# First attention of a hybrid kernel: VectorE takes additions and maxes in another place, and two products of the shared expert move into the last pair

## The reference

```
x = x + attn_a(layernorm(x))          # q, k, v, softmax(q k^T / sqrt(128)) v, w_o
logits = layernorm(x) @ router_w      # 4096 tokens, 8 experts
idx1, idx2 = first and second argmax of softmax(logits)
pos1 = cumsum(mask1) - mask1          # place of a token in its expert, in token order
pos2 = cumsum(mask2) - mask2 + sum(mask1)
expert_in = dispatch @ x              # at most 1280 tokens for an expert
y = combine @ (silu(expert_in @ w1 + b1) @ w2 + b2)
shared = silu(x @ sw1 + sb1) @ sw2 + sb2
x = x + y + 0.1 * shared
```

## Time and profile before

| | |
|---|---|
| median of 3 runs | 773.42 us |
| these runs | 767.63, 775.83, 773.42 us |
| the profiled execution | 770.89 us, span 769.1 us |
| mean granted clock of PE | 0.977 |
| PE busy | 704.7 us, 92% of the span |
| DVE busy | 523.9 us, 68% |
| ACT busy | 449.7 us, 58% |
| POOL busy | 440.9 us, 57% |

### The profile page before, as it was taken

The page is one execution under the profiler, slowest core; times in us unless marked ns, Lnnn a source line. Parts: engine busy times, 40 slices in busy tenths (PEclk is TensorE's granted clock), DMA queues, the critical chain, the costliest instruction groups (busy, mean ns, idle before and its releaser), DMA issues.

```text
span 769.1 us, 18168 instructions
## 1 busy us (share of the span) xinstructions
PE 704.7 (92%) x6152; PEld 641.6 (83%) x6152; DVE 523.9 (68%) x1665; ACT 449.7 (58%) x1144; POOL 440.9 (57%) x564
## 2 busy tenths in 40 slices
PE   6888789799999997889999998999999899999996
PEld 5777689799999996667777776777779899999996
DVE  5877765366556565768888988877676556655536
ACT  2565454344444443677878878787755444456545
POOL 6367777166666651344545767777777265666640
PEclk9999869999999998899999999999999999999999
DMA  7997111455556334333533434333201346555328
GB/s 245 309 323 183 46 48 55 58 113 108 108 99 133 78 104 118 104 99 109 142 101 91 126 119 147 100 95 111 62 30 53 53 84 131 109 97 112 90 68 287
DMA packets 167715, 89.35 MB, mean 116 GB/s; under 512 B 120576, under 2 KB 151890, under 8 KB 167528
## 3 DMA queue, kind: packets, MB, share of 16 engines
q1 hardware_dynamic: 155704, 69.89, 36.6%
q0 software_dynamic: 9216, 17.34, 6.6%
q10 hardware_dynamic: 2704, 0.98, 0.6%
HBM read 49.63 MB, written 39.67 MB: 116 GB/s over the span
## 4 chain that ended last, share of the span: by engine, by line
PE 57%; DVE 5%; POOL 5%; DMA 5%; SPq 4%; issue 4%; ACT 3%; ACTq 0%; DVEq 0%; POOLq 0%
PE bank L940 22%; PE bank L919 19%; PE bank L1021 4%; DMA qc<-qk_rows 3%; SPq L439 3%; POOL x_slots L611 3%; PE bank L980 2%; PE bank L998 2%; PE bank L1002 2%; POOL pt L695 2%; DVE negp L1951 1%; PE bank L976 1%; PE bank L981 1%; ACT pt L1389 1%; PE bank L1040 1%
## 5 line engine op out<-in xcount | busy, mean ns | idle before, releaser
L1291 ACT ACTIVATE hT<-bank,bias_T 128x256 f32<-128x256 f32 x448 | 175.7, 476 | 186.4 <-PE bank L919 186.3
L626 POOL DMA_INDIRECT y_rows<-yo,row_cur x160 | 158.5, 990 | 127.9 <-DVE yo L1845 103.2
L1951 DVE TENSOR_REDUCE negp<-bank 128x2 f32<-128x512 f32 (+1 forms) x192 | 129.6, 685 | 44.3 <-PE bank L981 27.1
L940 PE MATMUL bank<-w_s,hT 128*128 128x128 f32 x1280 | 155.9, 275 | 0.0
L611 POOL DMA_INDIRECT x_slots<-xr,slot_u x128 | 129.9, 1015 | 38.7 <-issue 35.5
L940 PEld LDWEIGHTS bank<-w_s,hT 128*128 128x128 f32 x1280 | 150.0, 192 | 0.0
L919 PE MATMUL bank<-xT_hl,w_hl 128*128 128x256 f32 x960 | 135.4, 291 | 9.1 <-DVE xT_hl L1719 9.1
L695 POOL TENSOR_SCALAR_AFFINE_SELECT pt<-pt 128x512 f32<-128x512 f32 x128 | 86.0, 680 | 92.7 <-ACT pt L1389 92.2
L1389 ACT ACTIVATE pt<-bank 128x512 f32<-128x512 f32 x192 | 107.8, 596 | 40.3 <-PE bank L1002 38.5
L919 PEld LDWEIGHTS bank<-xT_hl,w_hl 128*128 128x128 f32 x960 | 120.9, 192 | 9.6 <-issue 9.6
L1845 DVE TENSOR_TENSOR yo<-bank,b_b 128x256 f32<-128x256 f32 x80 | 33.9, 424 | 98.7 <-PE bank L940 98.7
(11 more groups left out here) (214 smaller groups left out, 1194.0 us busy)
## 6 DMA issues: line engine op xcount, KB each, us to landing
xg_all<-x_slots SPq DMA_DIRECT2D x316, 32.0 KB
w_s<-in_L_ffn_w SPq DMA_DIRECT2D x32, 256.0 KB
qk_rows<-qks SPq DMA_DIRECT2D x16, 512.0 KB, 3.6
bdk<-qk_rows SPq DMA_DIRECT2D x187, 32.0 KB
qc<-qk_rows SPq DMA_DIRECT2D x45, 128.0 KB, 2.8
x_slots<-xg_all SPq DMA_DIRECT2D x1, 5440.0 KB, 21.7
y_rows<-xg_all SPq DMA_DIRECT2D x1, 4096.0 KB, 14.3
yab<-y_rows SPq DMA_DIRECT2D x16, 256.0 KB, 3.3
```

Of the source, the lines that this page charges most:

```text
L626: pool.indirect_dma_start(y_rows, bass.IndirectOffsetOnAxis(ap=row_cur[:, g % ROWS, j:j + 1], axis=0), yo[:, g % RING, j, :], None, bounds ...
L940: m = pe.matmul(yb(w, l)[:, j * P:(j + 1) * P], hT[:, w % 2, f, j * P:(j + 1) * P], wt[:, f, :], start=(f == 0), stop=(f == FT - 1))
L1291: a = act.activation(hT[:, w % 2, f, :], HB[2 * (w % 2) + f // 2][:, (f % 2) * 256:(f % 2) * 256 + 256], ACT.Silu, bias=bias_T[:, b0 + f:b ...
L1951: dve.tensor_reduce(dst, AB[(g + k) % 2][:, :].rearrange("p (j k) -> p j k", j=heads), AX.X, ALU.max, negate=True).then_inc(S.amax_done, 1)
```

## The change

**In every pair, on DVE.** `maxes` of a pair's second sequence no longer stands at the start of the pair, but in the pair before, behind step 2 of `second` (`maxes(n + 3)`). `add_attn(n + 1)` moves from behind step 3 of `second` to ahead of step 0. Five steps of `second` now stand behind the maxes and `stats2_end`, where two stood. `placed` step 1 goes ahead of the first `norm_r`.

**In the last pairs.** `split_sw1` moves from the middle of pair 6 to the end of pair 5, `x_split(0, 0)` from pair 7 to the end of pair 6, `x_split(0, 1)` to behind the `norm_r` of pair 6. On PE `first_mm(0, 0)` and `first_mm(0, 1)` move into pair 7, on ACT `silus(0, 0)` too. What follows the last pair up to item 3 is written out in `attn_a_end`, one function for each engine, and the loop `moe` starts at item 4 (`START`).

```diff
--- before.py
+++ after.py
@@ -859,6 +859,8 @@
                     a_probs_transpose(n)
                 if 0 <= n + 1 < SEQS:
                     a_scores(n + 1)
+                if i == PAIRS - 1:
+                    first_mm(0, 0)
                 if 0 <= n + 2 < SEQS:
                     a_project(n + 2)
                 if valid(i):
@@ -874,6 +876,8 @@
                     a_scores(n + 2)
                 if valid(i - 1):
                     r_transpose(i - 1)
+                if i == PAIRS - 1:
+                    first_mm(0, 1)
                 if 0 <= n + 3 < SEQS:
                     a_project(n + 3)
                 if valid(i - 1):
...
@@ -942,21 +940,31 @@
                 m.then_inc(S.yo_done, 1)
 
             def moe(l, start, upto):
-                last = PAIRS * (l + 1) - 1
                 for w in range(start, upto):
-                    c = w - FRONT[l]
                     first_mm(l, w)
 
-                    if l == 0 and w == 1:
-                        r_logits(last)
                     if w > 0:
                         second_mm(l, w - 1)
-                    if l == 0 and w == 0:
-                        pe.wait_ge(S.pT_ready, SEQS)
-                        counts(last - 1, bank[5])
-                        r_transpose(last)
-                    elif l == 0 and w == 2:
-                        counts(last, bank[5])
+
+            def attn_a_end():
+
+                last = PAIRS - 1
+                second_mm(0, 0)
+                first_mm(0, 2)
+                pe.wait_ge(S.pT_ready, SEQS)
+                counts(last - 1, bank[5])
+                r_transpose(last)
+                second_mm(0, 1)
+                r_logits(last)
+                first_mm(0, 3)
+                second_mm(0, 2)
+                counts(last, bank[5])
+
+            for i in range(-2, PAIRS):
+                attn_a_pair(i)
+                if i == -1:
+                    pe.wait_ge(S.bias_in, 16 * 5)
+                    pe.transpose(R_[:, 0:38], bias_rows[:, :], ident[0:38, 0:38]).then_inc(S.bias_tr, 1)
 
             AB, CB, OB, MB, XB, ZB = bank[0:2], bank[2:4], bank[4], bank[5], bank[6], bank[7]
 
...
@@ -1262,6 +1271,8 @@
                     p_copy(n + 1)
                 if valid(i - 1):
                     r_copy(i - 1)
+                if i == PAIRS - 1:
+                    silus(0, 0)
                 if 0 <= n + 3 < SEQS:
                     g_copy(n + 3)
                 if 0 <= n + 2 < SEQS:
...
@@ -1306,15 +1317,10 @@
                     act.dma_start(xg[BLK * b:BLK * b + BLK, g % RING, :, :], by_block[:, :, BLK * b:BLK * b + BLK]).then_inc(gat[g % RING], 16)
 
             def moe(l, start, upto):
-                last = PAIRS * (l + 1) - 1
                 for w in range(start, upto):
                     if w == FRONT[l]:
                         first_chunk(l)
                     silus(l, w)
-                    if l == 0 and w == 0:
-                        r_copy(last)
-                    elif l == 0 and w == 1:
-                        gate_exps(last)
                     c = w - FRONT[l] - 24
                     if l == 1 and 0 <= c < 8:
 
@@ -1468,7 +1474,12 @@
                 silus(1, 2)
                 silus(1, 3)
 
-            moe(0, 0, ITEMS - 1)
+            silus(0, 1)
+            r_copy(PAIRS - 1)
+            silus(0, 2)
+            gate_exps(PAIRS - 1)
+            silus(0, 3)
+            moe(0, START, ITEMS - 1)
             act.wait_ge(S.init_b, 1)
             for i in range(-1, PAIRS):
                 attn_b_pair(i)
@@ -1723,15 +1734,17 @@
                 routed, led = valid(i - 2), valid(i - 1)
                 if valid(i):
                     inverse_sums(n)
-                if 0 <= n + 1 < SEQS:
-                    maxes(n + 1)
                 if valid(i):
                     add_attn(n)
-                for j in range(PLACED):
+                if routed:
+                    placed(i - 2, 0, bank[2])
+                for j in range(1, PLACED):
                     if routed:
                         placed(i - 2, j, bank[2])
-                    if led and j < 4:
-                        norm_r(i - 1, j)
+                    if led:
+                        norm_r(i - 1, j - 1)
+                if i == PAIRS - 1:
+                    x_split(0, 1)
                 if i == 0:
                     stats(4, 5)
                 if i < 0:
@@ -1761,33 +1774,30 @@
                         norm(i + 2, i + 3, j)
                 if i == -1:
                     stats(3, 4)
+                if valid(i):
+                    add_attn(n + 1)
                 if led:
                     second(i - 1, 0)
-                    second(i - 1, 1)
                 if valid(i):
                     stats2(i, 0)
                 if led:
-                    second(i - 1, 2)
-                    second(i - 1, 3)
-                if i == PAIRS - 2:
-                    split_sw1()
-                if i == PAIRS - 1:
-                    x_split(0, 0)
-                    x_split(0, 1)
-                if valid(i):
-                    add_attn(n + 1)
-                if led:
-                    second(i - 1, 4)
+                    second(i - 1, 1)
                 if valid(i):
                     dve.wait_ge(S.attn_added, n + 2)
                     stats2(i, 1)
                 if led:
-                    second(i - 1, 5)
+                    second(i - 1, 2)
+                if 0 <= n + 3 < SEQS:
+                    maxes(n + 3)
                 if valid(i):
                     stats2_end(i)
-                if led:
-                    second(i - 1, 6)
-                    second(i - 1, 7)
+                for j in range(3, SECOND):
+                    if led:
+                        second(i - 1, j)
+                if i == PAIRS - 3:
+                    split_sw1()
+                if i == PAIRS - 2:
+                    x_split(0, 0)
 
             for i in range(-2, PAIRS):
                 if i == -1:
@@ -1846,29 +1856,14 @@
                                   ).then_inc(S.yo_ready, 1)
 
             def moe(l, start, upto):
-                last = PAIRS * (l + 1) - 1
                 for w in range(start, upto):
                     c = w - FRONT[l]
-                    if l == 0 and w == 0:
-                        for j in range(4):
-                            norm_r(last, j)
                     if c == -1:
                         y_copy(l, w - 1)
-                    if w + 1 < ITEMS and not (l == 0 and w == 0):
+                    if w + 1 < ITEMS:
                         x_split(l, w + 1)
                         if 0 <= c + 1 < NCH:
                             rows_of(l, c + 1)
-                    if l == 0 and w == 1:
-                        for k in range(PLACED):
-                            placed(last - 1, k, bank[5])
-                        for k in range(LEAD):
-                            lead(last, k)
-                    elif l == 0 and w == 2:
-                        for k in range(SECOND):
-                            second(last, k)
-                    elif l == 0 and w == 3:
-                        for k in range(PLACED):
-                            placed(last, k, bank[5])
                     if l == 1 and w == ITEMS - 2:
                         tail_half(0)
                         tail_half(1)
@@ -2054,6 +2049,27 @@
                         if g == 3 and h == 1 and valid(i - 1):
                             stats2_end(PAIRS + i - 1)
 
+            def attn_a_end():
+                last = PAIRS - 1
+                for j in range(4):
+                    norm_r(last, j)
+                x_split(0, 2)
+                for k in range(PLACED):
+                    placed(last - 1, k, bank[5])
+                bias_add(0, 0)
+                y_copy(0, 0)
+                for k in range(LEAD):
+                    lead(last, k)
+                x_split(0, 3)
+                for k in range(SECOND):
+                    second(last, k)
+                y_copy(0, 1)
+                bias_add(0, 1)
+                x_split(0, 4)
+                for k in range(PLACED):
+                    placed(last, k, bank[5])
+                y_copy(0, 2)
+
             def attn_b_end():
                 t, n = PAIRS - 1, 2 * PAIRS - 1
                 for k in range(3):
...
```

More of the change, by code:

```diff
@@ L1293, in silus @@
                 a.then_inc(S.h_ready, 1)
+            for i in range(-2, PAIRS):
+                attn_a_pair(i)
+                if i == -1:
+                    act.wait_ge(S.bias_tr, 1)
+                    act.activation(bias_T[:, :], R_[:, 0:38], ACT.Copy).then_inc(S.bias_set, 1)
+            act.activation(bq_s[:, :], bias_T[:, 36:37], ACT.Copy, scale=HD ** -0.5)
             def first_chunk(l):
```

17 lines of the change are left out of this document (4 added, 13 removed).

## The result

The changed kernel takes 775.83 us, median of 20 runs (770.91 to 783.82), the kernel before 772.38 (767.63 to 778.16, 20 runs). The ratio is 1.0049 with a 95% interval of 1.0027 to 1.0070: slower by half a per cent, 3.5 us by the medians, where 2.6 us were forecast. The ratios in this document leave out two runs that count as slow, one of 783.82 us here and one of 786.31 us in experiment e4. The profiled execution of the changed kernel took 773.76 us with a span of 772.0.

A forecast was written before the change was run, and what follows sets the result against it. POOL's 64 dispatches were taken to bound the stage up to the first chunk. The last pair's +2.6 us on 770.89 gave 773.5 profiled; on the known executions' middle, 772.2, it gave 775 us, range 769.5 to 780.5.

The forecast's parts named there:

- What bounds the kernel: Up to the first chunk: the last of 64 dispatches on POOL, ending at 136.48 us, sets the chunk's `first_mm` at 142.99.
- A pair, forecast 0.15 us shorter: DVE's earlier maxes and additions: each pair gains 0.15 us, not 0.84; 0.7 us in five pairs, not passed to POOL.
- the walk: Step-by-step times of a pair from DVE's first `lead` step: maxes at 3.2 us, `second` ends 5.4, `norm_r` 7.6.
- `split_sw1` in pair 5, forecast nearly free: DVE, ahead of pair 5's `norm_r`: its 0.46 + 0.61 us nearly taken up by the 0.7 us gained and POOL's lag.
- The last pair, forecast +2.55 us to `rstd2_of`: Waits for the split and moved products, then ACT's loads: `rstd2_of` at 105.3 instead of 102.72 us, +2.6 in the sum.
- The clock: PE, last pair: lower level after the wait, `first_mm(0, 0)` 2.7 us; what follows from 95 us on at the upper level.
- The rival sum with a drain: ACT, two table switches ahead of the gates: draining by the skill page costs 2.8 us more, sum +5.4; no chance given.
- POOL's queue did not give way: Rival, faster: pairs 0.84 us shorter, POOL's waits vanish; -3.0, to -3.9 us at most, 769. 15%.
- stayed low: Rival: the clock stays low through the last pair, products and values take longer; 5.5 us in all, 777.7. 15%.
- stayed up: Rival: the clock doesn't fall, first product costs 1.5 us, ACT's gates bound the end of pair 7; +1.4, 773.6. 15%.
- The slots of the last pair: Rival, slower: pair 7's slots use up the 6.4 us margin and delay the last eight dispatches; up to 3 us, 781. 10%.
- pair 6's `lead` starts at 85.8, as before: DVE, after `split_sw1` in pair 5: start of pair 6 unchanged at 85.8 us (85.0 to 86.5).

The follow-up runs named there:

- e4: The changed kernel with `silus(0, 0)` behind `gate_exps(6)` on ACT: 778.77 us, ratio 1.0090 to the kernel before.
- e5: The changed kernel with POOL taking eleven ready dispatches ahead of `rstd2_of` in pair 7, without waits for PE between them: 774.31 us, ratio 1.0040 to the kernel before.
- e8: The changed kernel with the edits of e3 and e5 together, ten dispatches instead of eleven: 770.93 us, ratio 1.0000 to the kernel before.
- e10: e5 with SP issuing all four block loads of chunk 0 in layer 0: 772.00 us, ratio 1.0021 to the kernel before.
- e1: The changed kernel with products and silus back in place, input splits behind `norm_r` of pair 6; DVE's new order and `split_sw1` stay: 774.34 us, ratio 1.0029.
- e2: The changed kernel with DVE's pairs in the old order; `split_sw1`, products and splits as in the change: 779.48 us, ratio 1.0097 to the kernel before.
- e3: The changed kernel with each of the last pair's two products behind its `a_values` on PE: 774.15 us, ratio 1.0037 to the kernel before.
- e7: The changed kernel with 13 useless matmuls on PE ahead of `first_mm(0, 0)`, to keep the clock up: 774.20 us, ratio 1.0028 to the kernel before.
- e11: The changed kernel with SP issuing all four block loads of chunk 0 in layer 0: 776.09 us, ratio 1.0082 to the kernel before.
- e9: e8 with SP issuing all four block loads of chunk 0 in layer 0: 770.14 us, ratio 0.9990 to the kernel before.

## Why the prediction came out right, step by step

- **What bounds the kernel.** Confirmed: in the kernel before and in the change the last dispatch hands on the time, and nothing that the edit touches lies behind the chunk. It was incomplete: there is a second gate 1.8 us beneath the first one, seen in e5 to e8, and a third in e10. The chain of the earlier trace rows shows the last of the gates alone, and the description of the kernel names only SP's loads of the first chunk, where ACT issues two of the four blocks.
- **A pair, forecast 0.15 us shorter: wrong in sign.** DVE's `lead` steps of pairs 3 to 6 stood at 54.90, 65.10, 75.25 and 85.77 and now at 54.23, 64.62, 75.02 and 86.46: the pairs take 10.39, 10.40 and 11.44 us instead of 10.20, 10.15 and 10.52. DVE's timeline of pair 4, beside the earlier trace rows, and PE's behind it:

```profile
64.62 0.19 DVE L1554 TENSOR_REDUCE r<-bank 128x4 f32<-128x32 f32 x1 [1.83 <-PE bank L832]
...
67.96 0.69 DVE L1693 TENSOR_REDUCE negmax<-bank 128x2 f32<-128x512 f32 x1 [0.15 <-PE bank L793]
...
69.79 0.18 DVE L1597 TENSOR_TENSOR acc<-acc,cnt 128x16 bf16<-128x16 bf16 x1
69.89 0.16 DVE L1698 RECIPROCAL rsum<-psums 128x2 f32<-128x2 f32 x1
70.15 0.61 DVE L1705 SCALAR_TENSOR_TENSOR x<-bank,rsum,x 128x128 f32<-128x128 f32 x2
70.67 0.28 DVE L1606 TENSOR_TENSOR sel<-MK,bank 128x128 f32<-128x128 bf16 x1
70.99 0.28 DVE L1610 TENSOR_REDUCE RR<-sel 128x16 f32<-128x128 f32 x1
...
72.20 0.33 DVE L1539 TENSOR_SCALAR xr<-x,mv,rstd 128x128 f32<-128x128 f32 x1
```

```profile
70.33 0.63 PE L802 MATMUL bank<-ident,probs 128*128 128x128 f32 x4
70.80 1.03 PE L793 MATMUL bank<-xnT,gT 128*128 128x256 f32 x4
72.58 0.66 PE L825 MATMUL bank<-ident,xr 128*128 128x128 f32 x4 [0.76 <-DVE xr L1539]
```

  The maxes come 3.3 us after `lead` and the chain of `second` ends at 5.35, both as the walk had them (3.2 and 5.4), and PE's wait for the exponentials is gone. But the walk let the last `norm_r` end at 7.6, and it ends at 7.91. In the old order the maxes stood between the reciprocal and the addition that needs it, and the addition began 5.22 us after `lead` (it is the row behind the maxes of the earlier trace rows, at 70.32); now the reciprocal stands last in a chain of dependent steps, the addition waits for it 0.26 us from start to start and begins at 5.53, and the steps from there to the last `norm_r` take 2.38 us instead of 2.27. `r_transpose`, which had 0.15 us to spare, waits 0.76 for it. The forecast bounded the pair on the side of a gain and not on that of a loss, and it charged dependent steps (0.23 us each) in `second` alone. That the order costs the 0.2 us is shown by e1, which has it with the new order and without a product, and e2, whose pairs with the old order take 10.15 to 10.22 us. Why it costs them is read from the rows; no run separates it.
- **`split_sw1` in pair 5, forecast nearly free: it costs some 0.7 us.** The pair takes 11.44 us where it took 10.52, of which 0.2 are the order's, and PE's `r_transpose` waits 1.80 us instead of 0.76. No run has the new order without this split; in the old order it costs 2.65 us (e2). Both errors together are the +1.67 us to the `lead` in pair 6, and e1 shows that sum without a product (44.51 us). Forecast was 85.8, measured 86.46, in an execution that began a microsecond early.
- **The last pair, forecast +2.55 us to `rstd2_of`, measured +2.30.** From the `lead` in pair 6: split 5.2 us (5.7 forecast), `a_values(14)` begins 7.8 (8.4), `a_values(15)` ends 16.1 (16.2), gates 17.6 (17.75), statistics' end 19.2 (19.5). Of the named waits all are there. e3 prices the place ahead of the values at 1.9 us of dispatches, e4 that ahead of the gates at some 1.0 us of `rstd2_of` (63.76 against 62.71; e11, with the changed kernel's last pair, has 63.36), e7 the clock at 1.3 us of `rstd2_of`.
- **The clock.** It fell in the wait and `first_mm(0, 0)` took 2.64 us (2.7 forecast); `a_values(14)` took 1.66, between the 1.14 of the upper level and the 2.05 of the lower, as the granted clock rose from 0.50 to 1.00 between 95 and 96; from `counts` on all is at the upper level. The Trainium skill, "TensorE: Matmul & The Clock Gate", section "What's actually happening", has activity release the throttle; in this place the trace agrees. Behind the chunk's start it stays low for longer: `first_mm` takes 2.90 us there and the `second_mm` behind it 2.73.
- **ACT.** Two loads of 1.28 us, the first 0.01 us behind `r_copy`, the next work 0.02 and 0.01 us behind them. The rival sum with a drain of the Trainium skill, "ScalarE: Activation LUTs", section "What ACT_TABLE_LOAD costs", falls: the gates are there at 104.10 (103.55 forecast), not 2.8 us later.
- **The rivals.** POOL's queue did not give way. The clock neither stayed low nor stayed up. The slots of the last pair were early enough: `counts(7)` began at 121.00 (121.1 forecast) and POOL never waited behind 107. The products' own wait, which the forecast was built on, is the cause of the stage's loss: without the products the chunk starts as before (e1).
- **The sum.** +1.67 + 2.30 + 0.21 - 0.38 = +3.8 us from the first dispatch to the chunk, of which I had 2.6. The term of the last pair was sized right. The step that failed is "pair 6's `lead` starts at 85.8, as before": it nearly held in absolute time only because this execution began a microsecond early, and from the first dispatch it was off by 1.67 us. That the profiled execution came out at 773.76 us with 773.5 forecast is luck in this part: 1.2 us too little in the sum met 0.98 us by which the first dispatch came early. The medians differ by 3.5 us, so 775 for 775.83 is right in direction and mechanism and somewhat small in size.

## What to carry to other kernels

Work put into an idle gap of a pipeline costs what the instructions behind it in the queue hand on: place it behind the instruction that the bounding engine waits for, not ahead (e3 gave back 1.9 of 4.2 us), and let the bounding queue first take what is ready (e5: no wait left, 5.2 us). When consecutive dependent steps are interleaved with others, the others are their cover; to take them out can be a cost even if no instruction is added (0.2 us a pair here, the reason read from rows alone). Work moved on an engine costs least behind the step that another engine waits for: `split_sw1` cost 2.65 us ahead of the maxes and at most 0.9 behind them. Before you price an earlier finish of the bounding chain, look for what else the next stage waits for: here the places of ACT's loads and of DVE's addition behind PE's last item took 3 of 5 us.

## What the runs showed of the hardware

- With 2.73 us of extra matmuls in the idle gap (13 in the code, 23 records), the product behind them took 1.66 us, at the upper clock; without them 2.64.
- Four block loads took SP 1.80 us to issue in e10 and e11 and 2.53 in e9. Two took it 0.82 in the change (1.41 in e8), beside 0.88 for ACT's two. The chunk came 0.9 us later with all four on SP's queue, in e9 against e8 and in e11 against the change.
- From the first of ACT's two block loads to the transposition passed 3.0 to 3.6 us where both engines' loads left together (before, the change, e1 to e4), and from the second of them 2.2 to 2.6 us where ACT's left last (e5 to e8).
